# Graph transformer layer on one core: the gates' bias moves from TensorE to VectorE, with new step orders on every engine

## The reference, cut to what matters

```python
h = relu(layernorm(x))
x = x + attention(h, adj)              # 6 heads of 64: q, k, v, masked softmax, @ Wf + bf
h = relu(layernorm(x))
x = x + gat(h, adj)                    # 12 heads of 32
# inside gat:
h_a = h @ W_a                          # per head ("heads")
attn = softmax(mask(leaky(tanh(h_a) @ w_src + (tanh(h_a) @ w_dst).T)))
feat_out = elu(attn @ h_a + b)
gate = sigmoid(h @ H_w.T + H_b)        # the gates; H_b is the bias that the change moves
return gate * feat_out + (1.0 - gate) * h
```

## Time and profile before

| | |
|---|---|
| time of three runs | 1309.01, 1311.48, 1311.65 us, median 1311.48 |
| profiled execution, first to last instruction | span 1309.3 us |
| what lies around the span | the page gives no time of its own for it; the span stands inside the runs' 1309.01 to 1311.65 |
| busy share of the span | PE 97%, ACT 96%, DVE 92%, POOL 70% |
| DMA | 33.74 MB, 7.7% of 16 engines for the data queue |

### The profile page before, as it was taken

The page is one execution under the profiler, slowest core; times in us unless marked ns, Lnnn a source line. Parts: engine busy times, 40 slices in busy tenths (PEclk is TensorE's granted clock), DMA queues, the critical chain, the costliest instruction groups (busy, mean ns, idle before and its releaser), DMA issues.

```text
span 1309.3 us, 33375 instructions
## 1 busy us (share of the span) xinstructions
PE 1265.7 (97%) x10511; PEld 918.9 (70%) x10511; DVE 1209.1 (92%) x4401; ACT 1251.5 (96%) x3701; POOL 913.2 (70%) x1106
## 2 busy tenths in 40 slices
...
DMA packets 29854, 33.74 MB, mean 26 GB/s; under 512 B 10481, under 2 KB 29681, under 8 KB 29681
## 3 DMA queue, kind: packets, MB, share of 16 engines
...
## 4 chain that ended last, share of the span: by engine, by line
PE 88%; ACT 3%; DVE 3%; POOL 2%; DMA 1%; issue 1%; SPq 1%; POOLq 0%; DVEq 0%; ACTq 0%
PE job L623 27%; PE pt L696 18%; PE job L635 14%; PE unit L670 7%; PE job L718 7%; PE job L764 6%; PE job L611 4%; PE unit L687 3%; PE job L773 2%; ACT p L874 1%; DMA xb<-in_x_dram 1%; PE job L619 1%; POOL prod L1282 1%; ACT pT L884 1%; DVE y L1051 1%
## 5 line engine op out<-in xcount | busy, mean ns | idle before, releaser
L874 ACT ACTIVATE p<-y,min 128x256 f32<-128x256 f32 x768 | 394.1, 539 | 0.9 <-DVE min L1125 0.8
L1119 DVE SCALAR_TENSOR_TENSOR unit<-unit,s,dst 128x256 f32<-128x256 f32 x768 | 335.8, 482 | 14.0 <-issue 1.7
L696 PE MATMUL pt<-ident,p 128*128 128x128 f32 x2304 | 331.5, 275 | 12.3 <-ACT p L874 7.1
L623 PE MATMUL job<-w,h 128*128 128x384 f16 x1728 | 311.1, 326 | 1.8 <-DVE h L1024 1.7
L696 PEld LDWEIGHTS pt<-ident,p 128*128 128x128 f32 x2304 | 268.3, 142 | 42.9 <-ACT p L874 14.0
L1125 DVE CUSTOM_DVE_ANT_0 y<-unit,mask 128x256 f32<-128x256 f32 x768 | 290.5, 414 | 0.0
L1260 POOL TENSOR_SCALAR p<-p,rec 128x256 f32<-128x256 f32 x384 | 178.7, 481 | 123.3 <-DVE rec L1058 122.9
L623 PEld LDWEIGHTS job<-w,h 128*128 128x128 f16 x1728 | 168.6, 98 | 97.3 <-DVE h L1024 2.5
L884 ACT ACTIVATE pT<-pt 128x512 f32<-128x512 f32 x384 | 232.3, 624 | 1.6 <-PE pt L696 1.6
L635 PE MATMUL job<-h,w 128*128 128x256 f16 x1728 | 216.4, 274 | 2.3 <-DVE h L1024 2.1
L830 ACT ACTIVATE p<-y,min 128x256 f32<-128x256 f32 x384 | 191.0, 503 | 13.8 <-PE pt L696 7.9
...
## 6 DMA issues: line engine op xcount, KB each, us to landing
...
```

Source lines behind the costliest of these rows:

```text
L623: last = mm(bank[:, 0:H], rows[:, i, c, t * P:(t + 1) * P], w16[:, w, j, c, :], start=n == 0, stop=(c, i, j) == (NC - 1, *TERMS[-1]))
L696: last = nc.tensor.transpose(pt_ps[u % 2][:, (2 * hh + kt) * P:(2 * hh + kt + 1) * P], probs[:, u % 3, hh, kt * P:(kt + 1) * P], ident[:])
L874: last = op(p1[:, u % 3, hh, :], y1[:, u % YB, hh, :], ACT.Exp, bias=min1[:, u, hh:hh + 1], scale=-1.0, accum_out=sum1[:, t, h:h + 1])
L1119: V.scalar_tensor_tensor(leaky[:, hh * T:(hh + 1) * T], bank[:, hh * T:(hh + 1) * T], s8[par][:, t, h:h + 1], dst5[:, c % 2, hh, :], ALU.a ...
```

## The change

1. GATE on PE loses its bias matmul (L619): nine matmuls a half and no tenth. The tensors `ones_b`, `gate_b3`, `gate_part` and two of the three GATE_BIAS steps go.
2. VectorE evacuates each half of GATE from PSUM and adds the scaled bias row; ScalarE does one tanh per batch, in place, from SBUF, 128 x 768.
3. Every list of steps is a new one (STARTING, ORDERS, ENDING, and SP's repeated part begins one repetition earlier).
4. The semaphore that counted evacuated `pt` banks becomes two, one for each bank, so that PV0 and PV1 wait on two. EXP0 and EXP1 wait for the transpose that read their own buffer (three units before) instead of the third transpose before it in PE's list. Waits that other waits implied are written out: SP's mask load waits for MASK0 too, STATS0, AGGREGATE1, RSTD0, RSTD1 and SKIP each name what they overwrite.

```diff
@@ orders, the repeated part of PE and DVE (the others change in the same manner) @@
 ORDERS = {
     "PE": steps("""
-        B PV1 0, P QK 0, L LN_T0 0, B PT1 9, B PT1 10, P QK 1, A GATE 1, B PT1 11, P QK 2, L LN_T0 1, P PT0 0,
...
+        L LN_T0 0, B PV1 0, P QK 0, B PT1 9, B PT1 10, P QK 1, B PT1 11, A GATE 1, P PT0 0, L LN_T0 1, B PV1
...
@@ transposed probabilities @@
+        def prob_bank(b, step, u):
+
+            n = n_t.before(b, step, u)
+            return pt_ps[n % 2], s_pT[n % 2], n // 2
...
             def load_adj(b, par, _):
                 adj_b = adj_v[b.ref]
                 if b.ref >= 2:
-                    used = n_mask1.after(b.back(2), "MASK1")
-                    sp.wait_ge(s_mask1, used)
+                    sp.wait_ge(s_mask0, n_mask0.after(b.back(2), "MASK0"))
+                    sp.wait_ge(s_mask1, n_mask1.after(b.back(2), "MASK1"))
...
-            def to_rows(bank, rows, t, w, bias=False):
+            def to_rows(bank, rows, t, w):
 
                 n = 0
-                if bias:
-                    mm(bank[:, 0:H], ones_b[:], gate_b3[:], start=True, stop=False)
-                    n = 1
...
+            def wait_evacuated(b, step, u):
+
+                for unit in (u - 1, u):
+                    _, evacuated, used = prob_bank(b, step, unit)
+                    pe.wait_ge(evacuated, used + 1)
...
             def pv0(b, par, i):
-                pe.wait_ge(s_pT, n_t.after(b, "PT0", (3, 5)[i]))
+                wait_evacuated(b, "PT0", (3, 5)[i])
...
             def exp1(b, par, u):
                 c, t = divmod(u, 2)
                 act.wait_ge(s_y1, n_y1.after(b, "SCORES1", u))
-                if n_t.some_before(b, "PT1", u, 2):
-                    act.wait_ge(s_t, n_t.before(b, "PT1", u, 2))
+                if u >= 3:
+                    act.wait_ge(s_t, n_t.after(b, "PT1", u - 3))
+                elif b.ref >= 1:
+                    act.wait_ge(s_t, n_t.after(b.back(1), "PT1", u + 9))
...
-            def gate_(b, par, t):
-                bank, taken = made(b, "GATE", t)
-                if t == 0 and b.ref >= 1:
-                    act.wait_ge(s_gate, n_gate.after(b.back(1), "GATES"))
-                op(gtanh[:, t, :], bank[:, 0:H], ACT.Tanh, scale=post_g[:]).then_inc(taken, 1)
+            def gate_(b, par, _):
+                for t in range(NT):
+                    _, _, taken, value = job(b, "GATE", t)
+                    act.wait_ge(taken, value)
+                op(gtanh[:], gtanh[:], ACT.Tanh, scale=post_g[:]).then_inc(s_gtanh, 1)
...
+            def gate_(b, par, t):
+                bank, taken = made(b, "GATE", t)
+                if b.ref >= 1:
+                    dve.wait_ge(s_gate, n_gate.after(b.back(1), "GATES"))
+                V.tensor_tensor(gtanh[:, t, :], bank[:, 0:H], gate_b_row[:], ALU.add).then_inc(taken, 1)
```

More of the change, by code:

```diff
@@ L80 @@
[L80 to L89, removed]
@@ new lines @@
+        LN_T0 0 4, LN_T0 1 4, QK 1 3, PT1 9 1, GATE 1 2, PT1 10 1, PT1 11 1, QK 2 3, PV1 0 1, PT0 0 3, PT0 1
+        3, DST_T 0 2, PV1 1 1, DST 0 2, PT0 2 3, OUT_T 0 1, OUT_T 1 1, Q 0 4, DST 1 2, PT0 3 3, K 0 4, PV0 0
+        3, DST 2 2, PT0 4 3, PT0 5 3, V 0 4, PV0 1 3, PT1 0 2, PT1 1 2, K 1 4, OUT0 0 3, OUT0 1 3, DST 3 2,
+        PT1 2 2, DST 4 2, Q 1 4, PT1 3 2, Q 2 4, V 1 4, LN_T1 0 3, LN_T1 1 3, PT1 4 2, PT1 5 2, DST 5 2, K 2
+        4, PT1 6 2, HEADS 0 3, HEADS 1 3, PT1 7 2, GATE 0 3, PT1 8 2
@@ new lines @@
+        GATE 0 1, SCORES1 11 0, GATE 1 1, SCORES0 0 2, SCORES0 1 2, SCORE_SUM 0 1, NORMP0 0 2, SCORES0 2 2,
+        SCORES0 3 2, NORMP0 1 2, STATS0 0 4, DST_T 0 1, NORMP0 2 2, PV1 0 0, SCORES0 4 2, NORMP0 3 2, RECIP1
+        0 0, SCORES0 5 2, SCORES1 0 1, PV1 1 0, NORMP0 4 2, SCORES1 1 1, NORMP0 5 2, LN_T0 0 3, LN_T0 1 3,
+        PV0 0 2, SCORES1 2 1, SCORES1 3 1, PV0 1 2, K 0 3, SCORES1 4 1, OUT_T 0 0, SCORES1 5 1, OUT0 0 2,
+        OUT_T 1 0, SCORES1 6 1, OUT0 1 2, STATS1 0 2, STATS1 1 2, SKIP_H 0 1, AGGREGATE1 0 2, SCORES1 7 1, K
@@ new lines @@
+        1 3, K 2 3, SCORES1 8 1, LN_T1 0 2, LN_T1 1 2, SCORES1 9 1, SCORES1 10 1, SCORES1 11 1, GATE 0 2,
+        FINISH 0 0, SCORES0 0 3, FINISH 1 0, SCORES0 1 3, SCORES0 2 3, LN_T0 0 4, LN_T0 1 4, NORMP0 0 3,
+        SCORE_SUM 0 2, NORMP0 1 3, GATE 1 2, SCORES0 3 3, SCORES0 4 3, NORMP0 2 3, PV1 0 1, DST_T 0 2,
+        SCORES0 5 3, NORMP0 3 3, PV1 1 1, RECIP1 0 1, OUT_T 0 1, OUT_T 1 1, SCORES1 0 2, NORMP0 4 3, SCORES1
+        1 2, NORMP0 5 3, K 0 4, SCORES1 2 2, SCORES1 3 2, PV0 0 3, SKIP_H 0 2, PV0 1 3, SCORES1 4 2, K 1 4,
@@ L166 @@
+        1, P QK 2, A DST_T 0, P PT0 1, B OUT_T 0, B OUT_T 1, P PT0 2, A DST 0, A DST 1, L Q 0, P PT0 3, L K
+        0, L K 1, P PT0 4, P PT0 5, P PV0 0, P PV0 1, A PT1 0, A DST 2, A PT1 1, L Q 1, P OUT0 0, P OUT0 1,
+        A PT1 2, A PT1 3, A DST 3, A DST 4, L V 0, L V 1, A PT1 4, L Q 2, P LN_T1 0, P LN_T1 1, A DST 5, A
+        PT1 5, L K 2, A PT1 6, P HEADS 0, A PT1 7, P HEADS 1, P GATE 0, A PT1 8
     """),
     "ACT": steps("""
-        B PT1 8, B EXP1 10, B EXP1 11, A GATE 0, L LN_T0 0, P EXP0 0, P EXP0 1, B PT1 9, B PT1 10, A GATE 1,
```

306 lines of the change are left out of this document (148 added, 158 removed).

## The result

The change makes the kernel slower: 1334.51 us median of four runs (1334.35 to 1335.34), against 1310.84 us (1309.01 to 1311.65, four runs) before, a ratio of 1.0182 with a 95% interval from 1.0167 to 1.0196. The forecast of 1297.7 us and its range were wrong.

What follows compares the result with a forecast made beforehand. TensorE's number of matmuls was taken to bound the middle. Savings of 11.8 us there, 1.5 at the start and 0.5 at the end from the profiled 1309.3 gave 1295.5, hence a 1297.7 us median; range 1289 to 1305.

Steps and rivals of the forecast that it cites:

- New waits and moved steps ... All these I cost at nothing: Reordered steps and added waits on all engines: claimed free, with a bound of 0.1 us each repetition, 3 us.
- GpSimd is idle 30% of the span: GpSimd: its idle share, given where the later GATES behind RES_ROW was costed at nothing.
- TensorE's -0.33 us for the bias matmuls: TensorE, middle: two bias matmuls fewer, 0.17 us each, save 0.33 us a repetition.
- The -0.10 for one entry less into the narrow form: TensorE, middle: full-array work enters narrow forms (QK, PV0, PV1) four times instead of five, saving 0.10 us a repetition.
- rival 3: TensorE: every tiling mode change costs the same, 0.30 us instead of 0.10 for the one that goes; 1292 us, chance 0.09.
- In the middle TensorE waits for nobody now: TensorE before the change: no waits in the middle, so no sign of saved matmuls turning into waits; that rival's chance 0.04.
- I cost the adds at nothing: VectorE: two adds, 0.92 us a repetition, hidden by TensorE; without that cover 25 us is on the path.
- one over 768 columns ... 0.74 us: ScalarE: the single tanh from SBUF takes 0.74 us, read from L898, which has that size.
- 0.22 forecast: ScalarE: two tanh of 0.48 us replaced by one of 0.74, 0.22 us less a repetition, saving nothing by itself.
- Rival 1: ScalarE takes over as bound, its idle 0.43 us all staying: a repetition of 38.73 us, 1303.5 us; chance 0.15.
- Rival 2: VectorE takes over as bound, waits for TensorE moving elsewhere: a repetition of 39.3 us, 1319 us; chance 0.06.
- Start and end: Outside the middle: start gains 1.5 us (bounds -4 and +2), end gains 0.5 us (bounds -3 and +2).

Runs made afterwards that it cites:

- run 1: The changed kernel with GpSimd's ELU_BIAS put back behind NORMP0 4 and 5, nothing else: 1312.36 us, 1.0014 of the kernel before.
- run 5: The kernel before with one edit, GpSimd's ELU_BIAS moved ahead of NORMP0 4 and 5: 1328.33 us, 1.0126 of the kernel before.
- Run 8: The kernel before with the new gates in the old lists and waits, tanh on only one column of each half: 1303.43 us, 0.9935 of before.
- run 10: The kernel before with new gates and waits, old lists, EXP0 2 and the tanh moved into ScalarE's gaps, VectorE's GATE 1 ahead of SCORE_SUM: 1304.87 us.
- run 11: The changed kernel with ELU_BIAS put back behind NORMP0 5, and VectorE's two adds cut to one column each: 1305.92 us, 0.9962 of before.
- run 3: The kernel before with only the gates changed (no bias matmul, two adds, one tanh), old lists and waits: 1314.50 us, 1.0026 of before.
- run 2: The changed kernel's lists and waits with the old gates (bias matmul, two tanh from PSUM, no adds): 1332.53 us, 1.0170 of before.

## Why the prediction was wrong

- **"New waits and moved steps ... All these I cost at nothing": this step failed.** It named GATES behind RES_ROW and MASK0 at the end of GpSimd's list, and passed over ELU_BIAS, which had moved past NORMP0 4 and 5. Its price: 39.867 - 39.019 = 0.85 us a repetition, 22 us, all but 2 of the loss (run 1); alone it costs 16 us (run 5). The argument "GpSimd is idle 30% of the span" was no cover. The question was not how much GpSimd has to do, but what it waits for with NORMP0 queued behind: a late input of 0.60 us and 1.8 us of work.
- **TensorE's -0.33 us for the bias matmuls was right** (0.31, runs 8 and 10). **The -0.10 for one entry less into the narrow form comes out near right, by the estimate below, but the new order pays it back by a wait that I had at nothing.** It is at QK 1, from run 1 on (TensorE, then VectorE):

```profile
607.24 1.09 PE L701 MATMUL pt<-ident,p 128*128 128x128 f32 x8
608.38 1.14 PE L674 MATMUL unit<-kT,qT 64*128 64x256 f32 x8
```

```profile
608.15 0.08 DVE L1058 DVE_READ_ACCUMULATOR2_ANT min<- 128x1 f32 x1
```

  QK 1 needs the bank that SCORES0 0 frees, 608.23, and SCORES0 0 needs QK 0. In the old list twelve transposes lie between QK 0 and QK 1, in the new one eight, since LN_T0 0 has moved ahead of PV1 0; they take 1.14 us, of which 0.12 is this wait. The rest is 0.87 for the eight, 0.06 more for the first behind QK and 0.09 for the way into QK. The waits can be taken off, as an estimate, by what each start comes late against the same pair of groups elsewhere. Run 11 (38.82) has 0.27 us for NORM1 and 0.12 at QK 1, which leaves 38.43. Run 8 (38.64) has 0.10 at PT1 6, for the bank of ScalarE's PT1 4, and 0.04 at LN_T1 1, which leaves 38.50. The new order is 0.07 us shorter, near the 0.10. By the Trainium skill (TensorEngine Tiling (Array Packing), Key Properties) a change of mode drains the engine. The trace agrees in that both ways cost, 0.09 us in and 0.06 out beside transposes; the 0.30 of rival 3 for the change that goes doesn't show.
- "In the middle TensorE waits for nobody now" was read from the page's idle time, and nearly true: the kernel before has those 0.10 us at PT1 6 and 0.03 at LN_T1 1 too, 0.13 of 38.95, covered by the tail of the matmul ahead.
- **VectorE: the size of the adds was right, the cover was not.** Each takes 0.47 us from start to start (0.46 forecast). "I cost the adds at nothing" fails in the new lists: taking them away brings 0.20 us (run 11). The prediction counted VectorE's work as fixed, 37.9 of 38.52 us. The new lists made the same instructions longer, by 0.34 us (FINISH) and some 0.7 (SCORE_SUM), because other GpSimd steps lie beside them.
- **ScalarE: "one over 768 columns ... 0.74 us" was too low.** The tanh takes 0.83 us to the next start, with an EXP0 behind it (run 3) or an LN_T0 (run 10). The forecast took it from L898, an instruction of the same size, but without the tanh's scale by partition (`post_g`). The Trainium skill (ScalarE: Activation LUTs, What ACT_TABLE_LOAD costs) says that each operand of one column by partition adds about 93 ns, whatever the function; with it 0.74 becomes 0.83, and the trace agrees. In the changed kernel it is 0.95 to the next start, but there ScalarE waits: PT0 1 (L849) begins 0.02 to 0.03 us behind the transposes that it reads (TensorE, then ScalarE).

```profile
623.07 0.66 PE L701 MATMUL pt<-ident,p 128*128 128x128 f32 x4
```

```profile
623.76 0.60 ACT L849 ACTIVATE pT<-pt 128x512 f32<-128x512 f32 x1
```

  The wait is covered by the tail of the tanh and shows as no idle time. In work ScalarE gains 2 x 0.48 - 0.83 = 0.13 us a repetition, for 0.22 forecast.
- **Rival 1 was true for the gates alone**, and still dearer than its 38.73: run 3 stands at 38.97. I had taken ScalarE's idle 0.43 us as all that could stay. It came to 0.7 us of waits for TensorE in run 3, of which another order of ScalarE's work fills 0.4 (run 10).
- **Rival 2 had the direction and not the mechanism.** It wanted VectorE's "waits for TensorE" to "move to other places instead of going". They went: 17.8 us from 200 to 979 us before, and none shown in the changed kernel, where VectorE waits 6.3 us for ScalarE's SCALED instead. The loss came over GpSimd, which it did not name, and at 1334 instead of 1319 us.
- **Start and end:** the first QK stands at 20.38 us instead of 24.92, and the start gains 2.7 us for 1.5 forecast. I had Q coming 0.8 us later than its 19.04; it begins at 17.00. From the last DST_T to the end it is 40.7 us, 38.4 before: 2.3 us lost for 0.5 gained. That goes with the new lists and not with the gates: it is 40.7 in run 2, with the old gates, and 38.4 in run 10, with the new ones.

The gain of the change is real, 0.31 us a repetition, and each set of lists hid it in its own way: the new ones by GpSimd's order (0.85 us), and behind that by three short waits of TensorE, with VectorE and GpSimd in each other's way; the old ones by ScalarE's order. TensorE's waits at LN_T1 0, DST_T and QK 1 come to 0.21 + 0.15 + 0.12 us a repetition in run 1, and all of its waits in run 10 to 0.14. How the 0.38 us between the two divide by cause, beyond the 0.20 of the adds and the 0.06 of FINISH, is not settled.
